# Batch norm folded into the last weights by GpSimd instead of VectorE

## What is computed

```python
x = x + L0(_gn(x))    # channel norm, 1x1 q/k/v, depthwise 3x3, linear attention, silu, 1x1, channel norm
x = x + L1(_gn(x))    # 1x1 qkv, depthwise 5x5 and grouped 1x1, relu linear attention, 1x1 w_proj, batch norm
```

```python
out = jnp.einsum('bchw,oc->bohw', out, w_proj)
inv = bn_gamma / jnp.sqrt(bn_var + BN_EPS)
out = out * inv[None, :, None, None] + (bn_beta - bn_mean * inv)[None, :, None, None]
```

## Time and profile before

| what | value |
|---|---|
| time, median of three runs | 305.61 us |
| lowest and highest run | 305.22 and 307.94 us |
| the profiled execution's span, first to last instruction | 304.5 us |
| TensorE busy | 252.1 us (83%) |
| VectorE busy | 221.8 us (73%) |
| ScalarE busy | 154.8 us (51%) |
| GpSimd busy | 112.5 us (37%) |

### The profile page before, as it was taken

How to read it: one execution, slowest core, us unless ns; L and a number is a source line. 1 busy time by engine, 2 the same in 40 slices (tenths; PEclk the granted TensorE clock), 3 DMA queues, 4 the chain that set the end, 5 groups by cost and what they waited for, 6 DMA issues and landing times. The chain is left out here.

```text
span 304.5 us, 12524 instructions
## 1 busy us (share of the span) xinstructions
PE 252.1 (83%) x5285; PEld 190.5 (63%) x5285; DVE 221.8 (73%) x673; ACT 154.8 (51%) x397; POOL 112.5 (37%) x319
## 2 busy tenths in 40 slices
PE   0448799669795779896598999997999999889995
PEld 0335577448473558675467676776679877566761
DVE  5667687719999748798776867652678888766674
ACT  1355974849972266866339327651343337822320
POOL 8165455008676344774415222220212221343100
PEclk9999999979999999999779999999999999999999
DMA  7620079970000200000002745638000000002212
GB/s 226 136 48 9 0 186 219 215 149 4 4 4 2 68 2 5 2 2 0 1 2 46 167 99 114 153 65 206 4 2 4 4 4 2 2 4 71 71 53 87
DMA packets 15177, 18.61 MB, mean 61 GB/s; under 512 B 3841, under 2 KB 8961, under 8 KB 15121
## 3 DMA queue, kind: packets, MB, share of 16 engines
q1 hardware_dynamic: 13440, 17.23, 23.5%
q10 hardware_dynamic: 1680, 0.58, 0.9%
HBM read 3.54 MB, written 2.20 MB: 19 GB/s over the span
## 5 line engine op out<-in xcount | busy, mean ns | idle before, releaser
L1163 PE MATMUL bank<-cin,tband 64*32 64x240 f32 (+5 forms) x2632 | 83.0, 402 | 9.1 <-ACT tband L604 3.5
L1163 PEld LDWEIGHTS bank<-cin,tband 64*32 64x32 f32 x2632 | 63.9, 107 | 27.0 <-issue 10.0
L604 ACT ACTIVATE tband<-tband,row_edge 128x96 f32<-128x96 f32 (+1 forms) x96 | 31.5, 391 | 33.6 <-POOL tband L460 32.8
L1159 PE MATMUL bank<-ident,rings 128*128 128x128 f32 x192 | 32.5, 299 | 15.7 <-ACT rings L556 7.4
L966 DVE STREAM_TRANSPOSE cpos<-bank 64x256 f32<-64x256 f32 x88 | 39.4, 447 | 5.4 <-PE bank L1163 4.2
L1159 PEld LDWEIGHTS bank<-ident,rings 128*128 128x128 f32 x192 | 23.1, 151 | 29.6 <-issue 10.7
L908 DVE STREAM_TRANSPOSE cin<-bank 128x768 f32<-128x768 f32 x32 | 31.0, 976 | 9.5 <-PE bank L1163 9.5
L496 POOL TENSOR_SCALAR ring_v<-cpos,mask_b 128x512 f32<-128x512 f32 x30 | 20.9, 710 | 35.2 <-PE bank L1163 20.7
L556 ACT ACTIVATE rings<-bank,ln_b,ln_s 128x128 f32<-128x128 f32 x64 | 24.3, 470 | 9.3 <-POOL ln_b L448 9.2
L460 POOL TENSOR_TENSOR tband<-taps,pw 128x160 f32<-128x160 f32 x24 | 10.6, 462 | 39.8 <-PE bank L1163 39.8
L969 DVE STREAM_TRANSPOSE cpos<-bank 128x256 f32<-128x256 f32 x52 | 19.5, 419 | 7.0 <-PE bank L1163 6.7
(11 more groups left out here) (144 smaller groups left out, 445.3 us busy)
## 6 DMA issues: line engine op xcount, KB each, us to landing
cin<-cin SPq DMA_DIRECT2D x48, 192.0 KB, 4.2
cin<-cin SPq DMA_DIRECT2D x18, 128.0 KB, 3.5
xin<-in_x_dram SPq DMA_DIRECT2D x4, 512.0 KB, 6.4
out_dram<-rings SPq DMA_DIRECT2D x16, 128.0 KB, 1.8
taps<-tap_rows SPq DMA_DIRECT2D x16, 30.0 KB
taps<-tap_rows SPq DMA_DIRECT2D x16, 18.0 KB
cin<-cin ACTq DMA_DIRECT2D x2, 128.0 KB, 2.9
rings<-in_L_conv_w_qkv_dram SPq DMA_DIRECT2D x1, 192.0 KB, 8.5
```

The source lines that it names most:

```text
L604: last = a.activation(dst[:, :, 1 + e], dst[:, :, 0], ACT.Copy, scale=row_edge[:, e:e + 1])
L1159: last = t_.transpose(tile(dst, xl), src(xl), ident[:, :])
L1163: return t_.matmul(dst, stationary, moving, start=start, stop=stop, skip_group_check=True)
```

## The change

The fold becomes part of GpSimd's program. It stands between band 3 and band 4 of the first convolution, waits for the eight weight loads that SyncE issued, and uses GpSimd's own form of the reciprocal square root, which is split out of `layernorm` so that both call it. It is 17 instructions there: one for variance plus epsilon, 11 for the root, one for `inv`, two multiplications of `w_proj`, two for the bias. A new buffer `bn_tmp` of three columns holds its intermediate values, and a new semaphore `s_fold` tells TensorE and ScalarE. VectorE loses its 15 instructions and two waits.

```diff
--- before.py
+++ after.py
@@ -119,6 +119,7 @@
         vecs = sb("vecs", [P, 6])
         bn_inv = sb("bn_inv", [P, 1])
         bn_bias = sb("bn_bias", [P, 1])
+        bn_tmp = sb("bn_tmp", [P, 3])
         gstats = sb("gstats", [P, B, 6])
         gmv = sb("gmv", [P, B, 2])
         gtmp = sb("gtmp", [P, 3, B])
@@ -176,7 +177,8 @@
         s_ident = sem("identity_ready")
         s_const = sem("block_masks_ready")
         s_mask = sem("small_masks_ready")
-        s_bnw = sem("bn_folded")
+        s_bnw = sem("pointwise_weights_spread")
+        s_fold = sem("bn_folded")
         s_wt = sem("weights_transposed")
         s_wte = sem("weights_out_of_psum")
         s_chain = sem("dve_chain")
@@ -425,13 +427,8 @@
 
             tap_rows()
 
-            def layernorm(n):
-
-                y, t = lnt[:, 0, :], lnt[:, 1, :]
-                scale, w, less = ln_s[:, n % 2, :], lnw[:, n % 2, 0, :], lnw[:, n % 2, 1, :]
-                pool.wait_ge(s_lmv, n + 1)
-                if n >= 1:
-                    pool.wait_ge(s_ln, n)
+            def rsqrt(dst, w, y, t, before_dst=None):
+
                 link(g.tensor_scalar(y.bitcast(I32), w.bitcast(I32), -0.5, RSQRT_MAGIC, ALU.mult, ALU.add))
                 link(g.tensor_tensor(out=t, in0=y, in1=y, op=ALU.mult))
                 link(g.tensor_tensor(out=t, in0=t, in1=w, op=ALU.mult))
@@ -442,10 +439,32 @@
                 link(g.tensor_scalar(w, t, H0, H1, ALU.mult, ALU.add))
                 link(g.tensor_tensor(out=t, in0=t, in1=w, op=ALU.mult))
                 link(g.tensor_scalar(t, t, H2, 1.0, ALU.add, ALU.mult))
-                if n >= 2:
-                    pool.wait_ge(s_nrm, n - 1)
-                link(g.tensor_tensor(out=scale, in0=t, in1=y, op=ALU.mult))
+                if before_dst:
+                    before_dst()
+                link(g.tensor_tensor(out=dst, in0=t, in1=y, op=ALU.mult))
+
+            def layernorm(n):
+
+                scale, w, less = ln_s[:, n % 2, :], lnw[:, n % 2, 0, :], lnw[:, n % 2, 1, :]
+                pool.wait_ge(s_lmv, n + 1)
+                if n >= 1:
+                    pool.wait_ge(s_ln, n)
+                rsqrt(scale, w, lnt[:, 0, :], lnt[:, 1, :],
+                      (lambda: pool.wait_ge(s_nrm, n - 1)) if n >= 2 else None)
                 g.tensor_tensor(out=ln_b[:, n % 2, :], in0=less, in1=scale, op=ALU.mult).then_inc(s_ln, 1)
+
+            def fold_batchnorm():
+
+                w, y, t = (bn_tmp[:, n:n + 1] for n in range(3))
+                pool.wait_ge(s_w, 16 * 8)
+                link(g.tensor_scalar(w, vecs[:, 5:6], EPS, 1.0, ALU.add, ALU.mult))
+                rsqrt(bn_inv[:, :], w, y, t)
+                link(g.tensor_tensor(out=t, in0=bn_inv[:, :], in1=vecs[:, 2:3], op=ALU.mult))
+                g.tensor_scalar(wst[9].rearrange("p (g s e) -> p g s e", g=2, e=HD1),
+                                wst[7].rearrange("p (s g e) -> p g s e", g=2, e=HD1), t, 1.0, ALU.mult, ALU.mult)
+                g.tensor_scalar(wst[8], wst[8], t, 1.0, ALU.mult, ALU.mult).then_inc(s_fold, 1)
+                link(g.tensor_tensor(out=w, in0=t, in1=vecs[:, 4:5], op=ALU.mult))
+                g.tensor_tensor(out=bn_bias[:, :], in0=vecs[:, 3:4], in1=w, op=ALU.subtract).then_inc(s_fold, 1)
 
             for i in range(PAIRS):
                 layernorm(i)
@@ -481,6 +500,8 @@
             pool.wait_ge(s_t0, 16 * WW)
             pool.wait_ge(s_mask, 1)
             for n in range(NS):
+                if n == TSLOTS:
+                    fold_batchnorm()
                 band0(n)
                 m = n - 2 - TSLOTS
                 if m >= 0 and m % 2 == 0 and m // 2 < NQ:
@@ -771,6 +792,7 @@
                 k_relu(i)
 
 
+            act.wait_ge(s_fold, 2)
             for i in range(PAIRS):
                 last = a.activation(xres[:, i, :], xres[:, i, :], ACT.Identity, bias=bn_bias[:, :])
             last.then_inc(s_xb, 1)
@@ -835,27 +857,6 @@
                 for t in range(3):
                     last = v.tensor_copy(pwrep[:, t], pwst[:, t, :].unsqueeze(1).broadcast_to([P, WW, CG]))
                 last.then_inc(s_bnw, 1)
-
-            def fold_batchnorm():
-
-                w, y, t = (newt[:, n, 0:1] for n in range(3))
-                yield link(v.tensor_scalar(w, vecs[:, 5:6], EPS, None, ALU.add))
-                yield link(v.tensor_scalar(y.bitcast(I32), w.bitcast(I32), -0.5, RSQRT_MAGIC, ALU.mult, ALU.add))
-                yield link(v.tensor_tensor(t, y, y, ALU.mult))
-                yield link(v.tensor_tensor(t, t, w, ALU.mult))
-                yield link(v.scalar_tensor_tensor(out=y, in0=t, scalar=N1 / N0, in1=y, op0=ALU.add, op1=ALU.mult))
-                yield link(v.tensor_tensor(t, y, y, ALU.mult))
-                yield link(v.scalar_tensor_tensor(out=t, in0=t, scalar=N0 * N0, in1=w, op0=ALU.mult, op1=ALU.mult))
-                yield link(v.tensor_scalar(w, t, N0 * H0, N0 * H1, ALU.mult, ALU.add))
-                yield link(v.tensor_tensor(t, t, w, ALU.mult))
-                yield link(v.scalar_tensor_tensor(out=bn_inv[:, :], in0=t, scalar=N0 * H2, in1=y,
-                                                  op0=ALU.add, op1=ALU.mult))
-                yield link(v.tensor_tensor(bn_bias[:, :], bn_inv[:, :], vecs[:, 2:3], ALU.mult))
-                yield v.tensor_scalar(wst[9].rearrange("p (g s e) -> p g s e", g=2, e=HD1),
-                                      wst[7].rearrange("p (s g e) -> p g s e", g=2, e=HD1), bn_bias[:, :], None, ALU.mult)
-                yield v.tensor_scalar(wst[8], wst[8], bn_bias[:, :], None, ALU.mult).then_inc(s_bnw, 1)
-                yield link(v.tensor_tensor(bn_inv[:, :], bn_bias[:, :], vecs[:, 4:5], ALU.mult))
-                yield link(v.tensor_tensor(bn_bias[:, :], vecs[:, 3:4], bn_inv[:, :], ALU.subtract))
 
             def gn_aggregate(c, b0, n):
                 for b in range(b0, b0 + n):
@@ -987,12 +988,8 @@
 
 
             dve.wait_ge(s_r0, 16)
-            dve.wait_ge(s_r1, 16)
-            fold = fold_batchnorm()
             for n in range(NS):
                 conv_out(n)
-                if n >= NS - 16:
-                    next(fold, None)
                 if n % 2 == 1 and n // 2 < NQ:
                     q_max(n // 2)
                 m = n - 9
@@ -1459,7 +1456,7 @@
                 if 1 <= step < PAIRS:
                     kq_transpose(step)
                 if step == 1:
-                    pe.wait_ge(s_bnw, 2)
+                    pe.wait_ge(s_fold, 1)
                     for k in range(2):
                         last = t_.transpose(tile(bank[6], k), wst[9 - k], ident[:, :])
                     last.then_inc(s_wt, 1)
```

## The result

| kernel | median (us) | lowest to highest | kernel before, same chip | ratio, 95% interval |
|---|---|---|---|---|
| changed, first measurement | 303.53 | 300.24 to 304.46 | 305.81 | 0.9887 [0.9848, 0.9925] |
| changed, second | 302.16 | 301.51 to 304.19 | 306.59 | 0.9862 [0.9832, 0.9892] |
| changed, third | 302.65 | 301.98 to 303.78 | 306.27 | 0.9884 [0.9849, 0.9919] |

The change makes the kernel 1.1 to 1.4% faster by the ratios, about 3.5 to 4.2 us; the medians lie 2.3, 4.4 and 3.6 us apart, where 5.0 were forecast. The first median lies 0.6 us above the stated range, the two later ones inside it. The ratios leave out two runs in the slow state, 307.39 us of E3 and 1258 us of the kernel before when it was measured again.

A forecast was written before the change was run, and what follows sets the result against it. VectorE, stalled behind GpSimd's `q_scale`, was taken to hold up TensorE's convolution sets; idle times (3.81), four tails of 0.24 and 0.28 made 5.05 us, so 305.6 - 5.0 = 300.6 us, range 299.2 to 302.9.

The forecast's parts named there:

- What bounds the stretch: First block's convolution sets: four two-input VectorE instructions stall about 1.5 us each behind GpSimd's `q_scale`, so TensorE waits.
- The fold on GpSimd costs nothing: Between bands 3 and 4: 17 instructions take 4.8 us in GpSimd's idle time, 51.1 to about 56; nothing is late.
- A collision of the two engines in the new place: Rival, chance 0.03: fold slows VectorE's last input transposes, set 0 is 2.3 us late, time 302.9 us.
- TensorE's own pitch takes over: Sets 12 to 23 run at 1.24 us each without late suppliers, ending at 98.18 instead of 103.23: 5.05 us gained.
- 0.28 from the last group: Last three sets on TensorE: 0.28 us counted in the 5.05 us gain, beside four idle times and four tails.
- The whole first attention shifts by the 5 us: Behind set 23: `conv_out(23)` and the key maximum hang on that set, so the attention starts 5 us earlier.
- a rival with a chance of 0.08: One more granted-clock drop behind the shifted stretch takes back at most 2.8 us, giving 303.4 us; chance 0.08.
- The signs of being wrong: TensorE still waiting for `conv_out` after set 17, set 0 later than 63.6, or longer stretches after the first attention begins.
- a late supplier: Rival, chance 0.10: another supplier binds TensorE's sets at 1.38 us each; gain 3.5 us, time 302.1 us.

The follow-up runs named there:

- E3: Kernel before, with the fold left on VectorE but done in one piece before set 0: 303.57 us, ratio 0.9915.
- E1: Kernel before, fold still on VectorE between the sets, each two-tensor-input instruction rewritten with one tensor input and a per-partition scalar operand: 302.85 us, ratio 0.987.
- E2: Changed kernel with four unused two-input one-column products put back on VectorE, behind conv_out 12, 13, 14 and 16: 306.28 us, ratio 0.9985.
- E6: Kernel before with six extra unused products on TensorE in its waits of the attention: 306.64 us, ratio 1.0002.
- E7: Kernel before with one-tensor-input folding on VectorE, six extra TensorE products in the attention and three ahead of set 0: 302.25 us, ratio 0.9858.
- E4: Changed kernel without its new buffer, the fold on GpSimd using VectorE's scratch tile instead: 302.7 us, ratio 0.9869.

## Why the prediction was right or wrong

**What bounds the stretch: right, and shown.** E1 takes the second input away and leaves everything else, E2 puts four such instructions back: 4.7 us less than before, and 4.5 us more than the changed kernel's 36.45. By the Trainium skill's rule on two SBUF inputs (SBUF — State Buffer, "Who interferes with whom") the trace agrees in both directions, 0.17 us against 1.47 to 1.77 us.

**The fold on GpSimd costs nothing: right.** It took 51.63 to 56.45, 4.8 us as estimated; the two multiplications took 0.41 us each, inside the bounds of 0.20 and 0.47. Band 4 is not later. A collision of the two engines in the new place does exist, at 0.14 us: VectorE's three copies beside the fold took 0.60 us, before 0.46 (0.56 to 0.60 in six profiles with the fold on GpSimd, 0.45 or 0.46 in four without). The input transposes took their 0.98 us as before. The 1.27 us that VectorE idles behind the copies hide it.

**TensorE's own pitch takes over: right, with two thirds of a microsecond missing.** Sets 12 to 23 go at 1.24 us, and no supplier was late. But the piece took 15.76 us where 98.18 - 83.06 = 15.12 were forecast. E3's piece, without interruptions, took 15.27; so 0.15 is the sum itself and about 0.5 the interruptions. The term that was mis-sized is "0.28 from the last group", counted as waiting that goes: it is an interruption inside set 23 that stays (0.29 us between two matmuls' starts before, 0.49 after), and with set 21 a second one appears that used to lie in a wait for VectorE. The other 0.17 us are in how set 12 begins (19.63 us behind set 0, before 19.46); that is spread and no effect of the change, for the second profile of the kernel before has 19.62. Together they turn 5.05 into 4.24.

**"The whole first attention shifts by the 5 us": wrong in size by the clock.** The rest of the span kept its 150.2 us. The attention kept its 49.9 in one of three profiles of the changed kernel and took 1.0 and 1.6 us more in two, where the granted clock fell a second time. That was a rival with a chance of 0.08, priced at 2.8 us at most; it came oftener and cheaper. Whether the change makes it likelier stays open: an early fall inside the attention is in four of the six profiles without VectorE's stalls and without extra products (near 135 us in the changed kernel twice and in E1, at 100 us in E3), in none of the three with the stalls, and in E6, which has the stalls, ahead of its extra products. Ten profiles are too few, and nothing was tried that holds the moment of the fall fixed.

**The signs of being wrong.** Two of them came up in the first profile: set 0 started at 63.99, later than 63.6, and the attention was longer. The second is the clock's. The first tells nothing: the kernel before started set 0 at 63.60 and 63.96, the changed one at 63.99, 63.42 and 62.51.

The medians are then 3.7 to 4.2 us in the sets, less up to 1.6 us now and then in the attention, and earlier or later by up to 1.1 us with the start of set 0. The second and third median lie in the upper half of the range, which was put there for a late supplier and a collision. Neither happened; that interruptions and the clock led to nearly the same number is luck.

## What to carry to other kernels

A tiny VectorE instruction with two tensor inputs from SBUF, started behind a GpSimd multiplication that reads SBUF, stood here until the multiplication was over: 1.47 to 1.77 us for one element per partition. Look for such rows that take over a microsecond and end with a GpSimd row; write them with a per-partition scalar operand, or put them where GpSimd is idle, before moving them to another engine: E1 and E3 removed as much from the sets as the change did. When a wait is removed, the next limit decides how much of it is gained: here an interruption that lay inside the wait.

## What was not expected of the hardware

In these traces TensorE's interruptions go by the count of its instructions, not by the work. In E7 they lie 126 or 127 matmuls apart, about 254 instructions with the weight loads. In the changed kernel they are at the first matmul of set 21 and the 32nd of set 23, again 127 apart; in E7, with six more matmuls ahead of the sets, they come five and six matmuls earlier in the sets. The page of the profile after counts 42 transfers of instructions with 0.69 MB on one queue:

```profile
q8 instruction: 42, 0.69, 1.0%
```

That is 16.4 KB each, and 254 instructions of one such block would be 65 bytes each. The whole program fits this: 5,285 matmuls, as many weight loads and TensorE's 177 sequencer instructions are 256 for each of the 42 transfers. So I read the interruptions as TensorE waiting for its next block of instructions, which it reaches sooner the fewer gaps it has: 0.2 to 0.9 us for two or three blocks in the changed kernel, and in E7, where the clock never fell, 0.23 to 0.81 us of idle time before most blocks.

The times of this queue's packets (16,384 bytes each), which the traces keep, bear it out. In E7 each of the eight interruptions in the sets ends 1.33 to 1.58 us after a packet has ended; at set 21 and set 23 in the changed kernel's three profiles, E1, E3 and E4 it is 1.28 to 1.56 us. The later the packet, the longer the gap: at set 21 0.15 us in E3, where the packet ended 1.38 us before the preceding matmul began, and 0.87 us in the third profile of the changed kernel and in E4, where it ended 0.67 and 0.69 us before. In E7, with little else to wait for, neighbouring interruptions end 3.6 to 4.2 us apart, while 127 matmuls take 3.3 us at 1.24 us a set. So there the blocks would set the pace, and a kernel that removes TensorE's other waits should expect to meet this one. It is still inferred from counts and times; no run changed the size or number of the instructions.
